# Attention and feed-forward with a 4-bit weight decode: both inputs also laid out by dimension, and decode steps of the first two attention steps moved later

## What is computed

```python
def xattn(text, features, Wq, bq, Wk, bk):         # text = layernorm(x), features = ctx
    Q = einsum('btx,dx->btd', text, Wq) + bq
    K = einsum('bpx,dx->bpd', features, Wk) + bk
    scores = einsum('btd,bpd->btp', Q, K) * scale
    return einsum('btp,bpd->btd', softmax(scores), features)
x = x + xattn(layernorm(x), ctx, Wq, bq, Wk, bk)
x = x + ffn(layernorm(x), ...)                     # silu(x Wg) * (x Wu), then Wd; hidden size 3584
```

## Time and profile before

| | |
|---|---|
| time, 3 runs | 1981.54 us median (1979.77 to 1982.28) |
| profiled execution | first to last instruction 1973.9 us; its whole time is not given apart from that |
| busy in it | PE 98%, DVE 83%, ACT 75%, POOL 20% |
| attention, 116.2 to 420.0 us | 303.8 us |
| DMA | 314.6 MB, mean 159 GB/s |

### The profile page before, as it was taken

One profiled execution on the slowest core, in us unless ns is written; L12 is line 12 of the kernel. 1 busy time (PEld: TensorE's weight loads), 2 busy tenths in 40 slices (PEclk: granted clock), 3 DMA queues, 4 the chain that ended last, 5 costly groups with the idle time before them and its releaser, 6 DMA issues.

```text
span 1973.9 us, 29877 instructions
## 1 busy us (share of the span) xinstructions
PE 1928.0 (98%) x9872; PEld 983.3 (50%) x9872; DVE 1637.0 (83%) x2758; ACT 1484.2 (75%) x2758; POOL 404.3 (20%) x600
## 2 busy tenths in 40 slices
PE   8989999989999999999999999999999999999999
PEld 3468878754444444444444444444444444444444
DVE  6757888986988988988988998898898898996963
ACT  3767886757889889889889889889899999900000
POOL 0022464441211211211211211111123222201110
PEclk9999999999999999999999999999999999999999
DMA  9112689683555555554544644645569899893562
GB/s 346 30 49 65 170 233 233 180 299 72 140 127 119 148 125 124 148 130 113 156 122 117 156 127 113 150 129 120 137 176 239 230 216 247 217 274 117 173 224 85
DMA packets 393626, 314.63 MB, mean 159 GB/s; under 512 B 327296, under 2 KB 327296, under 8 KB 391552
## 3 DMA queue, kind: packets, MB, share of 16 engines
q1 hardware_dynamic: 347360, 159.07, 35.2%
q0 software_dynamic: 44032, 153.65, 23.9%
q10 hardware_dynamic: 2080, 0.01, 0.1%
HBM read 154.31 MB, written 82.31 MB: 120 GB/s over the span
## 4 chain that ended last, share of the span: by engine, by line
PE 53%; ACT 22%; DVE 12%; issue 6%; DMA 1%; DVEq 0%; ACTq 0%; POOL 0%
PE ps L2125 38%; PE ps L2167 12%; ACT sq L346 7%; ACT sq L342 5%; ACT w L346 2%; DVE w L362 2%; ACT w L342 2%; PE ps L1494 1%; ACT halves L414 1%; PE ps L1569 1%; DVE tail L2277 1%; ACT tail L2198 1%; ACT T L1664 1%; PE ps L1533 1%; DVE tail L1219 1%
## 5 line engine op out<-in xcount | busy, mean ns | idle before, releaser
L2125 PE MATMUL ps<-T,wS 128*128 128x512 f16 x4704 | 1017.6, 379 | 4.1 <-DVE ps L2232 2.5
L2125 PEld LDWEIGHTS ps<-T,wS 128*128 128x128 f16 x4704 | 459.8, 98 | 558.4 <-issue 4.9
L346 ACT ACTIVATE sq<-sq 128x512 f32<-128x512 f32 x898 | 516.2, 627 | 0.0
L362 DVE SCALAR_TENSOR_TENSOR w<-sq,w 128x512 f32<-128x512 f32 x590 | 417.3, 707 | 109.5 <-ACT sq L346 99.6
L342 ACT ACTIVATE sq<-q 128x512 f32<-128x512 int32 x598 | 362.9, 631 | 49.6 <-DVE w L362 47.5
L2167 PE MATMUL ps<-T,tail 128*128 128x512 f16 x1584 | 345.0, 379 | 5.3 <-issue 2.1
L2167 PEld LDWEIGHTS ps<-T,tail 128*128 128x128 f16 x1584 | 154.6, 98 | 193.3 <-issue 5.9
L1533 PE MATMUL ps<-T 128*128 128x256 f16 x1536 | 174.1, 273 | 4.2 <-DVE T L1760 4.1
L2167 PE MATMUL ps<-T,wS 128*128 128x512 f16 x768 | 168.5, 379 | 1.0 <-DMA T<-halves 1.0
L430 DVE SCALAR_TENSOR_TENSOR halves<-w,halves 128x512 f16<-128x512 f32 x240 | 162.4, 686 | 6.4 <-ACT halves L414 6.2
L2073 POOL DMA_DIRECT2D keep_h<-tail x196 | 106.3, 542 | 295.7 <-DVE tail L2277 293.6
(11 more groups left out here) (226 smaller groups left out, 1936.8 us busy)
## 6 DMA issues: line engine op xcount, KB each, us to landing
keep_h<-tail POOLq DMA_DIRECT2D x196, 256.0 KB, 2.5
tail<-keep_h POOLq DMA_DIRECT2D x66, 512.0 KB, 5.0
wS<-keep_h POOLq DMA_DIRECT2D x32, 512.0 KB, 4.8
q<-in_L_ffn_down_q POOLq DMA_DIRECT2D x56, 256.0 KB, 4.2
q<-in_L_ffn_up_q POOLq DMA_DIRECT2D x52, 256.0 KB, 2.9
q<-in_L_ffn_gate_q POOLq DMA_DIRECT2D x48, 256.0 KB, 3.4
keep_x<-T SPq DMA_DIRECT2D x38, 256.0 KB, 3.2
T<-in_x SPq DMA_DIRECT2D x9, 1024.0 KB, 5.6
```

The source lines that it names most:

```text
L346: nc.scalar.activation(place, place, ACT.Square, bias=b, scale=a).then_inc(un.s_act, 1)
L362: nc.vector.scalar_tensor_tensor(out=out, in0=square_place(un, u, i - 1), scalar=FACTORS[i - 1][1], in1=un.w[:, buf, :], op0=ALU.add, op1= ...
L2125: last = nc.tensor.matmul(ps[:, bank, :], un.wS[:, z % SLOTS, a, kt, :], t.Tp[side][product][:, :, b, kt, :], start=fresh and n == 0, stop ...
```

## The change

The host passes `x` and `ctx` twice, once by rows (in the order of the old views) and once by dimension: `x_cols` and `ctx_cols` are, per batch, 128 partitions x 8 x 256 rows.

- `turn_keys` and, but for batch 0, `turn_x` are gone, with their evictions out of PSUM. `keysT` hi and lo are made in two halves of 128x1024 from `key_cols` (loaded by SP) on ACT (`keys_hi`, blocks 4 and 5) and DVE (`keys_lo`).
- `x_normalise` is gone. The raw transposed x of batch b + 1 (`xT`, loaded by SP) is normalised on POOL: two `x_scale` and two `x_shift`, 128x1024 float32 each, behind blocks 0 to 3, with 1/deviation and shift spread over the partitions in `norm`. PE spreads them (`turn_norm`, four transposes a step), ACT copies them (`norm_rows`). ACT's `x_hi` follows at blocks 3 and 6, DVE's `x_lo` behind it.
- `keys16` (by rows) is made one step later and in one buffer: `key_rows_hi(b-1)` on ACT at blocks 1 and 2, `key_rows_lo(b-1)` on POOL behind blocks 4 and 5. `attended(b-1)` waits for it as before.
- `turned_probs` and `probs_lo` move from block 1 to block 5, and `probs_lo` stands behind `x_lo(b+1, 1)`.
- `bias_dots(b)` now reads the raw rows of batch b, behind the residuals of step b and ahead of `key_max`; scale and shift are applied to its result.
- Decode: fewer steps in the first two attention steps, more in the others, `CREDIT` (12, 18) for (9, 14). Counted out, the DVE and ACT steps done are: after step 0, 11 and 25 before, 9 and 21 now; after step 1, 24 and 47 before, 16 and 35 now; after step 7, 47 and 82 before, 44 and 76 now. The two plans meet in the first dealt period of the feed-forward part.

```diff
-CREDIT, FULL, FORMS_END = (9, 14), (35, 50), 9
+CREDIT, FULL, FORMS_END = (12, 18), (35, 50), 9
...
             if phase < ATTEND_PHASES:
-                return (0, 0, 0, 5, 2, 2, 2, 2, 3, 2)[n], (10, 0, 0, 3, 2, 2, 2, 2, 6, 4)[n]
+                return (0, 0, 0, 4, 2, 1, 1, 1, 3, 2)[n], (9, 0, 0, 2, 1, 1, 1, 1, 4, 3)[n]
             if phase < 2 * ATTEND_PHASES:
-                return (0, 0, 0, 4, 2, 1, 1, 2, 2, 2)[n], (1, 1, 2, 2, 2, 2, 2, 2, 5, 3)[n]
+                return (0, 0, 0, 2, 1, 1, 1, 2, 2, 2)[n], (0, 0, 1, 1, 1, 1, 1, 2, 4, 3)[n]
             if phase < HIDDEN_PHASE - ATTEND_PHASES:
-                return (0, 0, 0, 0, 0, 0, 1, 1, 1, 1)[n], (1, 0, 1, 0, 0, 0, 1, 1, 2, 2)[n]
+                return (0, 0, 0, 1, 0, 1, 0, 1, 1, 1)[n], (1, 0, 1, 0, 1, 0, 1, 1, 3, 3)[n]
...
-    KEYS_HI_AT = (2, 3)
-    KEYS_LO_AT = (3, 4)
-    PROBS_AT = 1
-    KEYS_AT = range(4, 4 + XG)
+    KEYS_HI_AT, KEYS_LO_AT = (1, 2), (4, 5)
+    X_HI_AT, KEYS_T_AT = (3, 6), (4, 5)
+    PROBS_AT = 5
...
+        def load_key_rows(b):
+            wait(sp, s_klo, TB * b)
+            sp.dma_start(keys[:, :, :], t.ctx_t[:, TB * b:TB * (b + 1), :]).then_inc(s_krows, 16)
...
-            if b >= 2 and b + 2 < BATCH:
-                sp.wait_ge(s_xn, TB * b if b == 2 else TB * (b + 1))
-                sp.dma_start(x_feed(b + 2), t.x_t[:, TB * (b + 2):TB * (b + 3), :]).then_inc(s_xf, 16)
...
+            if more:
+                sp.wait_ge(s_ktlo, HALVES * (b + 1))
+                sp.dma_start(key_cols[:, :, :], t.ctx_cols[b + 1]).then_inc(s_keys, 16)
...
+            if b + 2 < BATCH:
+                sp.wait_ge(s_xlo, x_split(b + 1))
+                sp.dma_start(xT[:, :, :], t.x_cols[b + 2]).then_inc(s_xcols, 16)
...
+        def x_scale(b, h):
+            pool.wait_ge(s_xcols, 16 * b)
+            pool.wait_ge(s_norm, b)
+            nc.gpsimd.tensor_tensor(x_half(h), x_half(h), norm[:, 0:SEQ].rearrange("p (o t) -> p o t", o=1).broadcast_to([P, 4, SEQ]),
+                                    ALU.mult).then_inc(s_scaled, 1)
+        def x_shift(b, h):
...
                 nc.gpsimd.tensor_tensor(RT[:, 1, o, :], R32[:, o % R_RING, :], RT[:, 0, o, :], ALU.subtract).then_inc(s_rlo, 1)
+                if o < 4 and b < LAST:
+                    (x_shift if o % 2 else x_scale)(b + 1, o // 2)
+                if o in KEYS_LO_AT and b > 0:
+                    key_rows_lo(b - 1, KEYS_LO_AT.index(o))
                 if b >= 2 and o >= 5:
                     t_sum(nc, pool, t, b - 2, o - 5)
...
+                if b == 0 and o == 0:
+                    turn_norm(1)
                 if o == PROBS_AT and b > 0:
                     turn_probs(b - 1)
-                if o in KEYS_AT:
-                    turn_keys(b, o - KEYS_AT[0])
+                if o == PROBS_AT and b + 2 < BATCH:
+                    turn_norm(b + 2)
...
+        def x_hi(b, h):
+            act.wait_ge(s_shifted, HALVES * (b - 1) + h + 1)
...
+            nc.scalar.copy(xnT(b)[:, 0, 4 * h:4 * h + 4, :], x_half(h)).then_inc(s_xhi, 1)
...
+            if old:
+                t_lo(nc, dve, t, c, 0)
+            if more:
+                x_lo(b + 1, 1)
             if b > 0:
                 probs_lo(b - 1)
```

More of the change, by code:

```diff
@@ L1547, in step @@
                 attended(b - 1, 1)
-            if more:
-                turn_x(b + 1, 1)
-            else:
-                pe.wait_ge(s_ktlo, XG * BATCH)
+            if not more:
                 late_turn(nc, pe, t, 1)
@@ L1555, in step @@
                 attended(b - 1, 3)
-            if more:
-                turn_x(b + 1, 2)
-            else:
+            if not more:
                 late_turn(nc, pe, t, 2)
-            pe.wait_ge(s_ktlo, XG * (b + 1))
+            pe.wait_ge(s_ktlo, HALVES * (b + 1))
             if b > 0:
@@ L1665, in step @@
                                      bias=t.query_col[:, o:o + 1]).then_inc(s_rev, 1)
[L1666 to L1671 removed]
+                if b == 0 and o == 0:
+                    norm_rows(1)
+                if o in KEYS_HI_AT and b > 0:
+                    key_rows_hi(b - 1, KEYS_HI_AT.index(o))
+                if o in X_HI_AT and more:
+                    x_hi(b + 1, X_HI_AT.index(o))
+                if o in KEYS_T_AT:
+                    keys_hi(b, KEYS_T_AT.index(o))
                 if o == 0 and b >= 3:
@@ L1681, in step @@
             for g in range(3):
-                if more:
-                    x_hi(b + 1, g)
-                else:
+                if not more:
                     late_places_due(g)
@@ L1688, in step @@
                     t_hi(nc, act, t, c, 2 + g)
-            if more:
-                x_hi(b + 1, 3)
-            else:
+            if not more:
                 late_places_due(3)
                 late_hi(nc, act, t, 3)
+                for i in range(TB):
+                    key_rows_hi(LAST, i)
             streams.act.run(base + KT)
+            if b + 2 < BATCH:
+                norm_rows(b + 2)
             exponents(b, 0)
@@ L1843, in step @@
                 scales(c)
+            streams.dve.run(base + 3)
+            if more:
+                x_lo(b + 1, 0)
+            streams.dve.run(base + 4)
+            keys_lo(b, 0)
+            streams.dve.run(base + 5)
+            keys_lo(b, 1)
+            streams.dve.run(base + 6)
+            if old:
+                t_lo(nc, dve, t, c, 0)
+            if more:
+                x_lo(b + 1, 1)
             if b > 0:
                 probs_lo(b - 1)
-                if more:
-                    bias_dots(b + 1)
-            else:
-                dve.wait_ge(s_bias, 1)
-                bias_dots(0)
-            streams.dve.run(base + 3)
-            for g in range(XG):
-                keys_lo(b, g)
-                if old and g >= 2:
-                    t_lo(nc, dve, t, c, g - 2)
-                streams.dve.run(base + 4 + g)
-            if more:
-                x_lo(b + 1, 0)
-            else:
+            else:
+                row_terms()
+            if old:
+                t_lo(nc, dve, t, c, 1)
+            streams.dve.run(base + 7)
+            if not more:
                 late_lo(nc, dve, t, 0)
@@ L1863, in step @@
                 residual(b - 1, 1)
-            if more:
-                x_lo(b + 1, 1)
-            else:
+            if not more:
                 late_lo(nc, dve, t, 1)
```

268 lines of the change are left out of this document (141 added, 127 removed).

## The result

The changed kernel takes 2066.0 us (median, 2061.0 to 2066.7) beside 1981.9 us for the kernel before: 1.043 of its time, 95% interval 1.0402 to 1.0459. The forecast was 2023 us, range 1990 to 2047. The sign was right; the loss is 84 us where 42 were forecast, and the time lies 19 us above the upper end of the range. The profiled execution took 2066.3 us, of which the span is 2064.5.

What follows compares the result with a forecast made beforehand. PE was taken to bound attention, with POOL close to its limit. Steps of 28.5 + 43 + 5 x 45.4 + 37 + 10.2 (clock) gave 345.7 us for 303.8, so 1981.5 + 42 = 2023 us, range 1990 to 2047.

Steps and rivals of the forecast that it cites:

- the loop: Attention steps 2 to 6: POOL's reduction, x operations, ACT, DVE, `attended`, next maximum in series; 45.4 us a step for 37.6.
- the stretch: DVE operations with both inputs in SBUF slowed beside POOL: +1.1 us once per step, bounds 0 and 2.4.
- POOL's own order: POOL behind its reduction: four `RT` lo, four x operations, two pairs of `RT` lo and keys lo; 17.6 us a step.
- step 1: Second attention step: POOL free at 15 us, 17.6 more, 10.5 for `attended` and scores; 43 us for 38.3.
- step 7: Last attention step, no x operation: PE's own 33.6 us and 3.4 of waits; 37 us for 40.9.
- PE bounds attention before; POOL is close behind: Kernel before, attention: PE busy 35.9 of 37.6 us a step; POOL needs 32 of 37.
- Price of an x operation: Each 128x1024 float32 operation on POOL, four per step in steps 0 to 6: 2.4 us, between 2.13 and 3.1.
- The clock: PE's granted clock lower after idling ahead of `attended`: 1.7 us a step in steps 1 to 6, bounds 0 and 3.3.
- Moved decode and loads at nothing: Decode steps moved to the feed-forward part, and loads of x and context by dimension: no time added.
- Rival (a): Attention: POOL's order alone binds, ACT and DVE keep up, clock not lowered; 42.2 us a step, 1996 us; chance 0.14.
- rival (b): Attention: PE stays the bound and the time falls by 42 us to 1940 us; chance 0.05.
- rival (c): POOL's second gap, behind the reduction, costs nothing: 7 us off each step, 1972 us; chance 0.05.

Runs made afterwards that it cites:

- two kernels side by side: The changed kernel as it is, and the changed kernel with the old decode quotas and credit put back: 2064.59 and 2064.53 us, 1.0432 and 1.0436.
- `probs_lo` alone: Changed kernel with only the turn of the probabilities and `probs_lo` put back from block 5 to block 1: 2062.1 us, 1.0429.
- two others: Changed kernel with reduction moved from POOL to PE and DVE, x operations cut to 4 of 1024 columns: 2014.8 us; with `probs_lo` at block 1 too, 2000.1 us.

## What the forecast had right, and where it failed

The sign and the loop were right. The size was not: 2066 us lies outside the range, and the loss is twice the forecast's. The step that failed is the term for the stretch, "+1.1 once in the loop", with nothing for it in POOL's own order and in the steps 1 and 7, and with the hand-over to the feed-forward part left out of the sum. Steps 2 to 6 alone, with their +14.1 us, would have given 2038, inside the range; step 1 (+9.6), step 7 (+5.8) and the hand-over (+9) took it out.

- *PE bounds attention before; POOL is close behind.* Right: with its reduction taken off POOL the kernel before gets no faster (1.0021), though POOL gains 13.7 us a step.
- *The loop through reduction, x operations, ACT, DVE, attended and maximum.* Right in its order and in five of its terms, which came within 0.7 us. PE waits ahead of `attended` in every step from 1 to 6, 13.8 to 19.2 us where 8 to 13 were named as the sign; ACT waits at `x_hi`; the clock falls. The other signs were passed too: steps of 43 to 48 us (49.9), POOL busy for 65 to 80 us more (88).
- *Price of an x operation, 2.4 us.* Right when alone: 2.35. Beside DVE's operations an `x_shift` took up to 3.33, above the bound of 3.1.
- *"I take +1.1 once in the loop; bounds 0 and 2.4"*, and *POOL's own order, 17.6 us.* This is the step that failed. In step 3 one `x_lo` took 2.91 us and one L362 2.84 for 0.67, and POOL's operations lengthened in turn: its order took 22.3 us (261.56 to 283.86) for 17.6 and became the last input of `attended`, 1.5 us behind DVE. The mis-sizing was to count a stretch once where it meets every pair of neighbours on both engines. The rule of the Trainium skill (SBUF — State Buffer, Who interferes with whom), that of a DVE operation with two SBUF inputs and a GpSimd operation that reads SBUF the one that came second is blocked for the whole of the other, was weighed in the forecast against the row of 1.75 us, and the row was taken. These runs agree with the rule: with the reduction off POOL, `tensor_tensor` operations of 128x2 and 0.16 us took 2.26 and 2.28, until the end of the x operation beside them.
- *Step 1, 43 us and 1.7 for the clock.* It took 54.3, the largest miss of one step. POOL was free at 18.0 us of the step for the 15 taken, its order took 21.5 for 17.6, DVE was later by 1.7 still, and `attended` with the scores took 13.1 for 10.5. DVE's part is one unbroken run of such stretches, 16 us long, of which the loop's term for DVE, 3.5 us, held the end alone:

```profile
168.68 2.90 DVE L1816 TENSOR_TENSOR T<-T 128x1024 f16<-128x1024 f32 x1 [12.39 <-ACT T L1643]
171.51 1.15 DVE L375 SCALAR_TENSOR_TENSOR w<-q,sg 128x512 f32<-128x512 int32 x1
172.59 3.37 DVE L1837 SCALAR_TENSOR_TENSOR T<-T,k_in 128x1024 f16<-128x1024 f32 x1
175.87 1.15 DVE L362 SCALAR_TENSOR_TENSOR w<-sq,w 128x512 f32<-128x512 f32 x1
176.95 3.14 DVE L1837 SCALAR_TENSOR_TENSOR T<-T,k_in 128x1024 f16<-128x1024 f32 x1
180.01 1.15 DVE L362 SCALAR_TENSOR_TENSOR w<-sq,w 128x512 f32<-128x512 f32 x1
181.09 3.13 DVE L1816 TENSOR_TENSOR T<-T 128x1024 f16<-128x1024 f32 x1
184.15 0.68 DVE L1843 SCALAR_TENSOR_TENSOR tail<-ps,tail 128x512 f16<-128x512 f32 x1
```

- *The clock, 1.7 us a step.* `attended` took 7.9 for 5.24: 2.7. It was sized from a wait of 2.95 us, behind which six of twelve matmuls and a turn were slowed; behind the 15.7 us of step 3 the clock stayed at its lower level until 289 us, and 13 of the 24 matmuls were.
- *Step 7, 37 us.* 42.8, with 7.4 us of waiting for `probs_lo` that were not in the sum.
- *The hand-over to the feed-forward part.* Not in the sum at all. The last exponents wait for DVE's L1856, one operation of 128x1 that meets two keys lo of POOL in a row (492.62 to 496.83):

```profile
493.07 3.79 DVE L1856 SCALAR_TENSOR_TENSOR top_s<-mx,score_out,row 128x1 f32<-128x1 f32 x1
```

  PE then stands 5.9 us for them and does the last `attended` in 8.22 us. No run took this away: in all 16 profiles of kernels with the change PE stands 4.4 to 7.6 us there, and the 337th gate-up product comes 6 to 10 us later behind the first one than in the kernel before.

```profile
499.26 1.12 PE L1525 MATMUL ps<-ident,tail 128*128 128x128 f32 x4 [5.89 <-ACT tail L1669]
501.87 8.22 PE L1541 MATMUL ps<-T,tail 128*128 128x512 f16 x24 [1.49 <-DVE tail L1843]
```

- *Moved decode and loads at nothing.* The decode right, by two kernels side by side. For the loads, no engine waits for x or context by dimension in attention, and the time went with POOL's work while the loads stayed. One load was not at nothing: at the hand-over ACT waits 2.0 us for the context rows of batch 7, ahead of the keys hi and lo that L1856 then meets.

The miss, added up: steps 2 to 6 took 249.6 us for 235.5, +14.1; step 1 54.3 for 44.7, +9.6; step 7 +5.8; step 0 -0.7; together 28.8, which with the forecast's 41.9 is the measured 70.7. The hand-over adds 9 and makes it 79.3 at the 337th matmul. The two profiled spans are 90.6 us apart and not 84, so 11 us lie behind that matmul. The profiles of the kernel before differ by as much there: its feed-forward part, from the first gate-up to the last down product, takes 1549.7 us in its own profile and 1560.3 in that of the kernel before with its reduction off POOL. What these 11 us are stays open.

Rival (a) (POOL's order alone, 1996 us) was wrong in size but had seen that this order is the second chain; rival (b), PE as the bound, is excluded; rival (c), that the gap behind the reduction costs nothing, too: it stands ahead of L1467 as before, 7.3 us. Two sums beside the forecast do not come out: 45.4 less the stretch of 1.1 is 44.3 and not 43.3, and rival (a) at 2.13 us an operation is some 1989 us and not 1986. Neither bears on the miss.

## What to carry to other kernels

Before operations on SBUF are put on POOL beside DVE, take as upper bound for each its own time and its neighbour's full length, for every pair that can meet, and look for chains of tiny dependent operations on DVE: each link can cost a whole POOL instruction. When several chains of nearly the same length close a loop, an edit to one shows nothing (here 0 us for `probs_lo` alone, 11 to 15 behind two others), so take them away together before a cause is called innocent. Turns on PE that looked like waste had a second use: they put one input of DVE's subtraction in PSUM, and none of these was stretched by POOL: all 64 on turned x and keys (L1760, L1784) took 0.67 to 0.69 us. And look past the part that was changed: the loss at the hand-over stood in no sum and in no experiment.

## What the runs showed that was not expected

- A DVE operation on 128x2 takes 2.0 to 2.3 us for 0.16 beside a POOL operation of 128x1024, and one on 128x1 took 3.79 us for 0.22 beside two in a row. A chain of 17 of them grew from 3.4 to 12.9 us.
- `probs_lo`, with one input in PSUM, stayed at 0.68 us, in step 3 in the middle of a keys lo of POOL (280.76 to 283.86).
- Moving the x operations to DVE raised DVE's work and made the kernel 33 us faster.
